# A selective-scan stage: one product with C for both feature halves, one GpSimd product of dx and B, and TensorE's side work one step earlier

## The chip, the core and the metric

The kernel runs on one core of one Trainium2 chip. Its engines are PE (TensorE, with PEld for its weight loads), DVE (VectorE), ACT (ScalarE), POOL (GpSimd) and SP (SyncE, which issues the DMAs here). The metric is device time in microseconds for the whole program. The program is eight stages of a network; the change is in one of them, the selective scan.

## The reference, cut to what matters

The stage is a Mamba block on 2048 tokens of width 128. It has 256 inner features and 16 states for each feature. For every state `s` and every feature, a recurrence runs over the tokens:

```python
def step(h, inp):
    x_t, d_t, B_t, C_t = inp
    dA = jnp.exp(d_t[:, :, None] * A[None, :, :])
    h = dA * h + (d_t * x_t)[:, :, None] * B_t[:, None, :]
    y_t = jnp.einsum('bds,bs->bd', h, C_t)
    return (h, y_t)
...
y = _selective_scan(x_ssm, delta, A, B, C, Dp)     # + x * Dp
y = y * _silu(z)
out = jnp.einsum('ble,de->bld', y, out_proj_w)
```

`x_ssm` comes from a convolution over four tokens and a SiLU, `delta`, `B` and `C` from projections of `x_ssm`, and `z` from a projection of the block's input.

## The kernel before

The tokens are cut into 4 chunks of 512 (`c`), and the 256 features into two halves of 128 partitions (`d` = 0, 1). A chunk has 16 steps, one for each state (`s`; `g = 16 c + s`). Every engine runs its own list in program order and waits on semaphores.

One step goes through the engines like this:

- ACT: `exp(delta * A)` of both halves into two PSUM banks (L1712). Then it saves the last column of the step before (`save`, L1690), and does the ACT part of the side work.
- SP: loads row `s` of B, spread over the partitions, into a ring of four tiles `b_rows` (L1454), and in five of the steps a row of C (L1460).
- POOL: `dbx = dx * b_rows`, one instruction for each half (L1520), into a ring of four tiles, which are two steps. A half's product waits until the scan two steps back is done.
- DVE: two scans (L1821), one for each half, from the exponential, `dbx` and the saved state into `h`, which has two buffers. Then the product of `h` with the row of C, which TensorE has spread over the partitions in a PSUM bank: `hc = h * C`, one instruction for each half (L1833).
- PE: for each half, `hc` is added into a PSUM bank by a matmul with the identity (`add_up`, L1572). Between the two halves' matmuls it spreads C's row for the next step (`spread_c`, L1565). There is one bank for C, so the spreading waits for the products of the step before.

In the steps 1, 3, 7, 9 and 11 (`LOW_STEPS`), POOL multiplies the second half of `h` with C instead (`read_out`, L1495, two steps later), and PE adds that (`add_low`, L1578). So 11 steps of a chunk have two products on DVE (called pair steps below), and 5 have one (single steps).

Around this, side work for this chunk, for the chunk before and for the chunk after is put into the steps by hand. On DVE, at the end of a step: `finish` (L1777, y times the gate of z, chunk before) in step 0, `add_out` (L1783, into the residual, chunk before) in step 2, `gate_z` (L1765) in 3 and 4, `gate_x` (L1759, chunk after) in 6 and 8, `take_delta` (L1769, chunk after) in 12 and 13. On PE, after the step's `add_up`s: `find_z` (L1543) in 0 and 2, `project_out` (L1589, chunk before) in 1, the convolution of the chunk after in 3 to 6 (`convolve`, L1381, two of its four matmuls in each), `project_x` (L1400) in 7 and 9, `project_dt` (L1553, L1555) in 8, 10 and 11, `add_skip` in 13 and 14. ACT and POOL have their parts of the gates between: ACT opens the gate of z in step 2, POOL sums it in step 4 (`sum_z`, L1487), and ACT closes it in step 3 or 4, ahead of the exponentials of the next step.

PSUM banks are shared, and that is where some of the waits come from: `convolve` of the chunk after writes the bank from which `add_out` reads, and waits for it; `project_x` reads `xs`, which `gate_x` writes; the first `add_up` of a chunk waits until `finish` has read the sums of the chunk before.

Of the kernel before, what the change touches and what calls it, by code (L numbers as in the profile page):

```python
# [1262 lines left out]
def selective_scan(core, early_ctx, ln, following):  # L1263
# [6 lines left out]
    LOW_STEPS, C_RING = (1, 3, 7, 9, 11), 3  # L1270
# [143 lines left out]
    def rest(ctx):  # L1414
# [8 lines left out]
        zs = [sb(f"zs{d}", [P, CH]) for d in range(ND)]  # L1423
# [5 lines left out]
        dx = [[sb(f"dx{i}{d}", [P, CH]) for d in range(ND)] for i in range(2)]  # L1429
# [4 lines left out]
        dbx = [sb(f"dbx{i}", [P, CH]) for i in range(RING)]  # L1434
        b_rows = [sb(f"b_rows{i}", [P, CH]) for i in range(RING)]
        h = [sb(f"h{i}", [P, ND, CH]) for i in range(2)]
        hc = [sb(f"hc{d}", [P, CH]) for d in range(ND)]
        state = sb("state", [P, DS, ND])
        yT = [sb(f"yT{d}", [P, CH]) for d in range(ND)]
# [3 lines left out]
        @block.sync  # L1443
        def _(sp):
            for c in range(NC_):
                cols = slice(c * CH, (c + 1) * CH)
                if c:
                    store_b(sp, c)
                sp.wait_ge(b_stored, 16 * (c + 1))
                for s in range(DS):  # L1450
                    g = c * DS + s
                    if g >= RING:
                        sp.wait_ge(dbx_done, (g - RING + 1) * ND)
                    sp.dma_start(b_rows[g % RING][:],  # L1454
                                 b_dram[s:s + 1, cols].to_broadcast([P, CH])).then_inc(b_loaded[g % RING], 16)
                    if s in LOW_STEPS:
                        k = low_before(g)
                        if k >= C_RING:
                            sp.wait_ge(low_done, k - C_RING + 1)
                        sp.dma_start(c_rows[k % C_RING][:],  # L1460
                                     b_dram[DS + s:DS + s + 1, cols].to_broadcast([P, CH])).then_inc(
                                         c_loaded[k % C_RING], 16)

        @block.gpsimd
        def _(pool):
# [6 lines left out]
            def join(c):  # L1472
                pool.wait_ge(cut_line, 3 * c + 2)
                if c:
                    pool.wait_ge(dbx_done, ((c - 1) * DS + DS - 1) * ND)
# [13 lines left out]
            def read_out(g):  # L1489
                k = low_before(g)  # L1490
                pool.wait_ge(c_loaded[k % C_RING], 16 * (k // C_RING + 1))
                pool.wait_ge(scanned, (g + 1) * ND)
                if k >= 2:
                    pool.wait_ge(low_summed, k - 1)
                nc.gpsimd.tensor_tensor(low[k % 2][:], h[g % 2][:, 1, :], c_rows[k % C_RING][:],  # L1495
                                        ALU.mult).then_inc(low_done, 1)

            def weigh(c, d):
                pool.wait_ge(delta_done, ND * c + d + 1)
                nc.gpsimd.tensor_tensor(dx[c % 2][d][:], delta[c % 2][d][:], xs[c % 2][d][:], ALU.mult).then_inc(dx_done, 1)  # L1500
# [7 lines left out]
            for c in range(NC_):  # L1508
                pool.wait_ge(dx_done, ND * (c + 1))
                for s in range(DS):  # L1510
                    g = c * DS + s
                    for d in range(ND):
                        u = g * ND + d
                        if d == 1 and s - 2 in LOW_STEPS:
                            read_out(g - 2)
                        if u >= RING:
                            pool.wait_ge(scanned, u - RING + 1)
                        if d == 0:
                            pool.wait_ge(b_loaded[g % RING], 16 * (g // RING + 1))
                        nc.gpsimd.tensor_tensor(dbx[u % RING][:], dx[c % 2][d][:], b_rows[g % RING][:],  # L1520
                                                ALU.mult).then_inc(dbx_done, 1)
                    if s in (4, 5):
                        sum_z(c, s - 4)
                    elif c + 1 < NC_:
                        if s in (6, 8):
                            sum_x(c + 1, s // 2 - 3)
                        elif s == 13:
                            cut(c + 1)
                        elif s == 14:
                            join(c + 1)  # L1530
                        elif s == 15:
                            weigh(c + 1, 0)
                            weigh(c + 1, 1)
# [3 lines left out]
        def _(pe):  # L1537
# [30 lines left out]
            def add_up(c, s, d):  # L1568
                if s == 0 and c:
                    pe.wait_ge(y_done, ND * (c - 1) + d + 1)  # L1570
                pe.wait_ge(hc_done, high_before(c * DS + s) + d + 1)
                nc.tensor.matmul(core.ps[:, Y_BANK + d, :], core.ident[:], hc[d][:],  # L1572
# [11 lines left out]
            def project_out(c):  # L1584
                pe.wait_ge(y_done, ND * (c + 1))
                pe.wait_ge(delta_done, min(ND * (c + 1) + 1, ND * NC_))
                for k in range(TPC):
                    for d in range(ND):
                        last = nc.tensor.matmul(core.ps[:, O_BANK, k * P:(k + 1) * P], yT[d][:, k * P:(k + 1) * P],  # L1589
# [13 lines left out]
            for c in range(NC_):  # L1603
                spread_c(c, 0)
                for s in range(DS):
                    if s:
# [6 lines left out]
                    if s in (0, 2):  # L1613
                        find_z(c, s // 2)
                    elif s == 1 and c:
                        project_out(c - 1)
                    elif c + 1 < NC_:
                        if s in (3, 4):
                            convolve(pe, c + 1, 0, range(0, 2) if s == 3 else range(2, DCONV))
                        elif s in (5, 6):  # L1620
                            convolve(pe, c + 1, 1, range(0, 2) if s == 5 else range(2, DCONV))
                        elif s == 7:
                            project_x(pe, c + 1, 0)
                        elif s == 8:
                            project_dt(c + 1, 0, 0)
                        elif s == 9:
                            project_x(pe, c + 1, 1)
                        elif s == 10:
                            project_dt(c + 1, 0, 1)
                        elif s == 11:  # L1630
# [12 lines left out]
        def _(act):  # L1643
# [43 lines left out]
            def save(c, s):  # L1687
                g = c * DS + s
                act.wait_ge(scanned, (g + 1) * ND)
                nc.scalar.copy(state[:, s, :], h[g % 2][:, :, CH - 1]).then_inc(saved, 1)  # L1690
# [57 lines left out]
        def _(dve):  # L1748
# [14 lines left out]
            def gate_z(c, d):  # L1763
                dve.wait_ge(z_gated, ND * c + d + 1)
                nc.vector.tensor_tensor(zs[d][:], core.ps[:, Z_BANKS[d], :], z_gate[d][:], ALU.mult).then_inc(zs_done, 1)  # L1765
# [6 lines left out]
            def finish(c):  # L1772
                for d in range(ND):
                    dve.wait_ge(summed, high_before(DS * (c + 1) - 1) + d + 1)
                    if c:
                        dve.wait_ge(out_done, c)
                    nc.vector.tensor_tensor(yT[d][:], core.ps[:, Y_BANK + d, :], zs[d][:], ALU.mult).then_inc(y_done, 1)  # L1777
# [28 lines left out]
            for c in range(NC_):  # L1806
                for s in range(DS):
                    g = c * DS + s
                    for d in range(ND):
                        u = g * ND + d  # L1810
                        dve.wait_ge(da_done, u + 1)
                        dve.wait_ge(dbx_done, u + 1)
                        if g >= 2 and d == 1 and (g - 2) % DS in LOW_STEPS:
                            dve.wait_ge(low_done, low_before(g - 2) + 1)
                        elif g >= 2:
                            dve.wait_ge(hc_done, high_before(g - 2) + d + 1)
                        if g >= 2:
                            dve.wait_ge(saved, g - 1)
                        if c and s < 2:
                            dve.wait_ge(saved, g)  # L1820
                        nc.vector.tensor_tensor_scan(out=h[g % 2][:, d, :], data0=core.ps[:, A_BANKS[d], :],  # L1821
                                                     data1=dbx[u % RING][:], initial=state[:, s, d:d + 1],
                                                     op0=ALU.mult, op1=ALU.add).then_inc(scanned, 1)
                    dve.wait_ge(c_spread, g + 1)
                    for d in range(ND):
# [1297 lines left out]
```

## Time and profile before

| what | value |
|---|---|
| time, median of 3 runs (lowest to highest) | 1595.23 us (1588.64 to 1595.8) |
| the profiled execution: time, span | 1593.81 us, 1592.1 us |
| the scan stage in the trace | 853 to 1104 us |
| PE, DVE, ACT, POOL busy over the whole span | 93%, 85%, 58%, 20% |
| mean granted clock of TensorE, whole span | 0.965 |

The span is the time from the first to the last instruction of the core; the program's time is 1.71 us longer. Busy shares are means over eight stages with different limits: POOL's 20% is the mean of stages in which it has nothing to do and of the scan stage, in which it is busy most of the time. A timeline row gives an instruction's start, its duration (of all of a run of like instructions, if it ends in x2 and more), and in brackets how long its engine stood idle before it and what ended that. Two DVE instructions in a row with no wait between them overlap in the records: the second starts a little before the first one's end.

### The profile page before, as it was taken

The page shows a single profiled execution, that of the slowest core. Times are in us where ns is not written, and L with a number is a line of the kernel's source. Part 1 is how long each engine was busy: PE and PEld are TensorE (multiplying, and loading weights), DVE is VectorE, ACT ScalarE, POOL GpSimd, SP SyncE. Part 2 cuts the span into 40 slices and gives each one's busy share as a digit, 9 for nine tenths or more (in the row PEclk, how much of TensorE's full clock was granted, in tenths as well). Part 3 has the DMA queues.
Part 4 walks back from the last instruction along what each step waited for, and adds up shares of the span by engine and source line. Part 5 has one row for each costly group of instructions (what it writes and reads, how often), then busy time and mean ns, then how long its engine had stood idle before and what let it go on. Part 6 is the DMA issues. An engine that isn't in the chain of part 4 may idle for free. (4 is left out here: it accounts for less than half of the span.)

```text
span 1592.1 us, 28331 instructions
## 1 busy us (share of the span) xinstructions
PE 1487.0 (93%) x10635; PEld 786.2 (49%) x10635; DVE 1345.6 (85%) x2432; ACT 930.0 (58%) x1755; POOL 317.4 (20%) x370
## 2 busy tenths in 40 slices
PE   7999999999999999899997988977999999989899
PEld 3122222222222222488873333333888877869787
DVE  7999999999999999376657999998776668877686
ACT  3189999999999999632235665754332342222232
POOL 4200000000000000000016889885000110020100
PEclk8599999999999999899999999999999999999899
DMA  3341110000000001000003233330000012300123
GB/s 104 125 144 31 30 34 29 25 25 25 26 25 26 26 25 55 6 1 1 1 3 93 80 88 96 89 95 23 1 1 1 1 35 75 108 1 1 54 88 101
DMA packets 44274, 71.55 MB, mean 45 GB/s; under 512 B 11764, under 2 KB 18981, under 8 KB 43434
## 3 DMA queue, kind: packets, MB, share of 16 engines
q1 hardware_dynamic: 44138, 69.75, 15.0%
q8 instruction: 84, 1.38, 0.4%
q14 instruction: 52, 0.43, 0.1%
HBM read 61.92 MB, written 6.88 MB: 43 GB/s over the span
## 5 line engine op out<-in xcount | busy, mean ns | idle before, releaser
L917 DVE TENSOR_REDUCE row_max<-ps 128x1 f32<-128x1024 f32 x512 | 583.4, 1212 | 10.6 <-PE ps L703 10.5
L823 ACT ACTIVATE probs<-ps 128x512 f32<-128x512 f32 x944 | 506.2, 595 | 51.9 <-PE ps L718 35.5
L703 PE MATMUL ps<-k_stack,q_stack 48*128 48x512 bf16 x1024 | 325.6, 401 | 10.9 <-DVE row_max L917 6.6
L644 PE MATMUL ps<-probs,v_head 128*16 128x256 f32 (+1 forms) x3920 | 316.2, 395 | 1.1 <-issue 1.1
L718 PE MATMUL ps<-q_stack,k_stack 51*128 51x512 bf16 x944 | 286.8, 384 | 0.0
L703 PEld LDWEIGHTS ps<-k_stack,q_stack 48*128 48x128 bf16 x1024 | 58.9, 95 | 249.0 <-DVE row_max L917 221.8
L1114 ACT ACTIVATE x_gate<-ps 128x512 f32<-128x512 f32 x128 | 76.5, 599 | 178.0 <-PE ps L131 178.0
L644 PEld LDWEIGHTS ps<-probs,v_head 128*16 128x16 f32 x3920 | 65.6, 94 | 199.4 <-issue 102.4
L1821 DVE TENSOR_TENSOR_SCAN s_h<-ps,s_state,s_dbx 128x512 f32<-128x512 f32 x128 | 156.7, 1265 | 7.8 <-ACT ps L1712 7.7
L1572 PE MATMUL ps<-s_hc,ident 128*128 128x512 f32 x216 | 119.8, 641 | 46.0 <-DVE s_hc L1833 40.7
L1520 POOL TENSOR_TENSOR s_dbx<-s_dx,s_b_rows 128x512 f32<-128x512 f32 x128 | 159.6, 1274 | 9.9 <-DVE s_h L1821 9.3
L1160 DVE TENSOR_TENSOR x_hidden<-x_gate,ps 128x512 f32<-128x512 f32 x128 | 87.0, 685 | 50.1 <-PE ps L131 38.5
L1712 ACT ACTIVATE ps<-s_delta,s_a_neg 128x512 f32<-128x512 f32 x128 | 86.5, 688 | 66.6 <-DVE s_h L1821 66.2
L1073 PEld LDWEIGHTS ps<-w_w,x_hidden 128*128 128x128 f32 x1024 | 122.7, 192 | 5.3 <-issue 1.5
L1073 PE MATMUL ps<-w_w,x_hidden 128*128 128x128 f32 x1024 | 125.0, 275 | 0.0
L2230 ACT ACTIVATE y_gate<-ps 128x512 f32<-128x512 f32 (+1 forms) x72 | 43.1, 598 | 119.1 <-PE ps L131 119.1
L129 PE MATMUL ps<-x_x_high,x_w_high 128*128 128x512 f32 x256 | 107.0, 418 | 1.1 <-DVE x_hidden L1160 1.1
L1171 DVE SCALAR_TENSOR_TENSOR x_res<-ps,x_probs,x_res 128x128 f32<-128x128 f32 x256 | 72.0, 344 | 42.3 <-PE ps L1073 41.9
L131 PE MATMUL ps<-x_x_low,x_w_high 128*128 128x512 f32 x256 | 101.6, 397 | 0.0
L130 PE MATMUL ps<-x_x_high,x_w_low 128*128 128x512 f32 x256 | 100.5, 393 | 0.0
L1572 PEld LDWEIGHTS ps<-s_hc,ident 128*128 128x128 f32 x216 | 39.5, 200 | 107.1 <-DVE s_hc L1833 78.0
L548 POOL TENSOR_TENSOR neg_max_parts<-neg_maxT,by_one 128x32 bf16<-128x32 f32 x16 | 4.0, 252 | 402.2 <-DVE neg_maxT L910 402.2
(357 smaller groups left out, 2091.5 us busy)
## 6 DMA issues: line engine op xcount, KB each, us to landing
s_b_rows<-s_b_dram SPq DMA_DIRECT2D x64, 256.0 KB, 3.3
y_spread<-y_probs_dram SPq DMA_DIRECT2D x128, 128.0 KB, 3.0
s_c_rows<-s_b_dram SPq DMA_DIRECT2D x20, 256.0 KB, 4.5
q_stack<-q_parts_dram SPq DMA_DIRECT2D x30, 96.0 KB
k_stack<-k_parts_dram SPq DMA_DIRECT2D x30, 96.0 KB
w_w<-w_dram SPq DMA_DIRECT2D x1, 2048.0 KB, 8.1
q_stack<-q_parts_dram SPq DMA_DIRECT2D x30, 64.0 KB
k_stack<-k_parts_dram SPq DMA_DIRECT2D x30, 64.0 KB
```

Of the source, the lines that this page charges most:

```text
L129: nc.tensor.matmul(bank, self.w_high[:, u, cols], self.x_high[:, chunk], start=True, stop=False)
L130: nc.tensor.matmul(bank, self.w_low[:, u, cols], self.x_high[:, chunk], start=False, stop=False)
L131: return nc.tensor.matmul(bank, self.w_high[:, u, cols], self.x_low[:, chunk], start=False, stop=True)
L644: last = nc.tensor.matmul(core.ps[32 * c:32 * c + VROWS, O_BANK, cut], v_head[buf][:, kt, :], probs[:, m % RING, c * CH:(c + 1) * CH][:, cut],
L703: last = nc.tensor.matmul(core.ps[:, 2 * b + r, :], qst[buf][0:KROWS, u * P:(u + 1) * P], kst[buf][0:KROWS, key:key + CH], start=True, sto ...
L718: nc.tensor.matmul(core.ps[:, S_BANK + n % S_RING, :], kst[buf][HALF:ROWS, kt * P:(kt + 1) * P], qst[buf][HALF:ROWS, c * CH:(c + 1) * CH], ...
L823: nc.scalar.activation(probs[:, us % RING, c * CH:(c + 1) * CH], core.ps[:, S_BANK + n % S_RING, :], ACT.Exp).then_inc(exp_done, 1)
L917: nc.vector.tensor_reduce(mx[:, head % 2, u, b:b + 1], core.ps[:, 2 * b:2 * b + 2, :], mybir.AxisListType.XY, ALU.max).then_inc(max_done, 1)
L1073: last = nc.tensor.matmul(core.ps[:, DOWN + n % 2, k * P:(k + 1) * P], hidden[n % 2][:, half, k * P:(k + 1) * P], w["w3"][:, e, half, :], ...
L1520: nc.gpsimd.tensor_tensor(dbx[u % RING][:], dx[c % 2][d][:], b_rows[g % RING][:], ALU.mult).then_inc(dbx_done, 1)
L1572: nc.tensor.matmul(core.ps[:, Y_BANK + d, :], core.ident[:], hc[d][:], start=s == 0, stop=s == DS - 1).then_inc(summed, 1)
L1821: nc.vector.tensor_tensor_scan(out=h[g % 2][:, d, :], data0=core.ps[:, A_BANKS[d], :], data1=dbx[u % RING][:], initial=state[:, s, d:d + 1 ...
```

## The change

- `h` has three buffers in place of two, and `dbx` is a ring of three pairs in place of four single tiles.
- POOL makes `dbx` for both halves in one instruction, with B's row read twice. The first scan of a step waits for that one instruction. `read_out` comes after it; before, it stood between the two halves' products.
- DVE multiplies both halves with C in one instruction (`read_high`) in the pair steps. In every step this waits for both scans of the step, and for all the `add_up`s of the step before.
- `finish` is one instruction for both halves, into `zs`, and stands in step 1 between the two scans; before, it stood at the end of step 0.
- PE's side work: both `find_z` in step 0; `project_out` in step 1, now ahead of that step's `add_up`s; and the convolution, `project_x` and `project_dt` each one step earlier (2 to 5, 6 and 8, 7, 9 and 10).

The side work on DVE, ACT and POOL keeps its steps. The diff, cut to its core:

```diff
+    H_RING, PAIR_RING = 3, 3
@@ POOL
-                    for d in range(ND):
-                        u = g * ND + d
-                        if d == 1 and s - 2 in LOW_STEPS:
-                            read_out(g - 2)
-                        if u >= RING:
-                            pool.wait_ge(scanned, u - RING + 1)
-                        if d == 0:
-                            pool.wait_ge(b_loaded[g % RING], 16 * (g // RING + 1))
-                        nc.gpsimd.tensor_tensor(dbx[u % RING][:], dx[c % 2][d][:], b_rows[g % RING][:],
-                                                ALU.mult).then_inc(dbx_done, 1)
+                    if g >= PAIR_RING:
+                        pool.wait_ge(scanned, (g - PAIR_RING + 1) * ND)
+                    pool.wait_ge(b_loaded[g % RING], 16 * (g // RING + 1))
+                    nc.gpsimd.tensor_tensor(dbx[g % PAIR_RING][:], dx[c % 2][:],
+                                            b_rows[g % RING][:].unsqueeze(1).to_broadcast([P, ND, CH]),
+                                            ALU.mult).then_inc(dbx_done, 1)
+                    if s - 2 in LOW_STEPS:
+                        read_out(g - 2)
@@ PE
                 if c or s:
-                    pe.wait_ge(hc_done, high_before(c * DS + s))
+                    pe.wait_ge(hc_done, c * DS + s)
...
                 for s in range(DS):
+                    if s == 1 and c:
+                        project_out(c - 1)
                     if s:
                         add_up(c, s - 1, 0)
                         spread_c(c, s)
...
-                    if s in (0, 2):
-                        find_z(c, s // 2)
-                    elif s == 1 and c:
-                        project_out(c - 1)
+                    if s == 0:
+                        for d in range(ND):
+                            find_z(c, d)
                     elif c + 1 < NC_:
-                        if s in (3, 4):
-                            convolve(pe, c + 1, 0, range(0, 2) if s == 3 else range(2, DCONV))
-                        elif s in (5, 6):
-                            convolve(pe, c + 1, 1, range(0, 2) if s == 5 else range(2, DCONV))
-                        elif s == 7:
+                        if s in (2, 3):
+                            convolve(pe, c + 1, 0, range(0, 2) if s == 2 else range(2, DCONV))
+                        elif s in (4, 5):
+                            convolve(pe, c + 1, 1, range(0, 2) if s == 4 else range(2, DCONV))
+                        elif s == 6:
                             project_x(pe, c + 1, 0)
...
@@ DVE
+            def read_high(g):
+                dve.wait_ge(c_spread, g + 1)
+                dve.wait_ge(scanned, (g + 1) * ND)
+                if g:
+                    dve.wait_ge(summed, high_before(g))
+                if g % DS in LOW_STEPS:
+                    nc.vector.tensor_tensor(hc[:, 0, :], h[g % H_RING][:, 0, :], core.ps[:, C_BANK, :],
+                                            ALU.mult).then_inc(hc_done, 1)
+                else:
+                    nc.vector.tensor_tensor(hc[:], h[g % H_RING][:],
+                                            core.ps[:, C_BANK, :].unsqueeze(1).to_broadcast([P, ND, CH]),
+                                            ALU.mult).then_inc(hc_done, 1)
...
-                        dve.wait_ge(dbx_done, u + 1)
+                        if d == 0:
+                            dve.wait_ge(dbx_done, g + 1)
...
+                        if d == 1 and s == 1 and c:
+                            finish(c - 1)
                         nc.vector.tensor_tensor_scan(...).then_inc(scanned, 1)
-                    dve.wait_ge(c_spread, g + 1)
-                    for d in range(ND):
-                        u = g * ND + d
-                        if d == 1 and s in LOW_STEPS:
-                            continue
-                        dve.wait_ge(scanned, u + 1)
-                        last = g - 2 if d == 1 and (g - 1) % DS in LOW_STEPS else g - 1
-                        if g:
-                            dve.wait_ge(summed, high_before(last) + d + 1)
-                        nc.vector.tensor_tensor(hc[d][:], h[g % 2][:, d, :], core.ps[:, C_BANK, :],
-                                                ALU.mult).then_inc(hc_done, 1)
-                    if s == 0 and c:
-                        finish(c - 1)
-                    elif s == 2 and c:
+                    read_high(g)
+                    if s == 2 and c:
                         add_out(c - 1)
```

## Rows read from the trace of the kernel before

**Rows 1.** Windows, the scan stage: length, busy PE, PEld, DVE, ACT, POOL, clock, DMA.

```profile
853.00:1104.00 251.00, 205.24 (x493) 82.07 (x493) 236.06 (x269) 151.78 (x302) 217.83 (x180) 0.96 0.31 83
```

**Rows 2.** Waits of DVE in the scan stage: us in total, times, longest.

```profile
DVE s_h L1821 <- ACT ps L1712: 7.7, 5, 2.2
DVE s_hc L1833 <- PE ps L1565: 4.8, 5, 1.3
DVE s_zs L1765 <- ACT s_z_gate L1673: 1.0, 1, 1.0
...
DVE s_hc L1833 <- PE ps L1572: 0.7, 3, 0.2
```

**Rows 3.** Timeline of DVE, steps 10 to 12 of chunk 1: start, us, instruction.

```profile
957.28 2.45 DVE L1821 TENSOR_TENSOR_SCAN s_h<-ps,s_state,s_dbx 128x512 f32<-128x512 f32 x2
959.65 1.25 DVE L1833 TENSOR_TENSOR s_hc<-s_h,ps 128x512 f32<-128x512 f32 x2
960.83 2.45 DVE L1821 TENSOR_TENSOR_SCAN s_h<-ps,s_state,s_dbx 128x512 f32<-128x512 f32 x2
963.20 0.66 DVE L1833 TENSOR_TENSOR s_hc<-s_h,ps 128x512 f32<-128x512 f32 x1
963.77 2.45 DVE L1821 TENSOR_TENSOR_SCAN s_h<-ps,s_state,s_dbx 128x512 f32<-128x512 f32 x2
967.50 1.28 DVE L1833 TENSOR_TENSOR s_hc<-s_h,ps 128x512 f32<-128x512 f32 x2 [1.28 <-PE ps L1565]
```

**Rows 4.** Timeline of DVE ahead of the stage: the second waits for the first.

```profile
843.99 0.68 DVE L1787 TENSOR_TENSOR s_rest<-s_full,s_bc 96x512 f32<-96x512 f32 x1
...
844.71 0.42 DVE L1789 CAST s_mid<-s_rest 96x512 bf16<-96x512 f32 x1
```

**Rows 5.** Groups by line and form, DVE, same operation at two lengths.

```profile
L917 DVE TENSOR_REDUCE row_max<-ps 128x1 f32<-128x1024 f32 x512 | 583.4, 1212 | 10.6 <-PE ps L703 10.5
...
L2050 DVE TENSOR_REDUCE l_k_maxima<-ps 128x1 f32<-128x512 f32 x4 | 2.7, 686 | 0.2 <-PE ps L1931 0.2
```

**Rows 6.** Groups by line and form, GpSimd.

```profile
L1520 POOL TENSOR_TENSOR s_dbx<-s_dx,s_b_rows 128x512 f32<-128x512 f32 x128 | 159.6, 1274 | 9.9 <-DVE s_h L1821 9.3
...
L2609 POOL TENSOR_TENSOR g_span<-g_span 128x512 f32<-128x512 f32 x1 | 1.9, 1901 | 0.1
L2609 POOL TENSOR_TENSOR g_span<-g_f 128x1024 f32<-128x1024 f32 x1 | 1.9, 1893 | 4.8 <-DVE g_f L2834 4.8
```

**Rows 7.** Timeline of DVE and TensorE, step 14 of chunk 0.

```profile
909.31 1.26 DVE L1833 TENSOR_TENSOR s_hc<-s_h,ps 128x512 f32<-128x512 f32 x2
...
910.03 1.12 PE L1572 MATMUL ps<-s_hc,ident 128*128 128x512 f32 x2 [0.22 <-DVE s_hc L1833]
...
910.99 0.38 PE L1565 MATMUL ps<-s_bc,w_pick 96*128 96x512 bf16 x1
...
911.21 1.02 PE L1572 MATMUL ps<-s_hc,ident 128*128 128x512 f32 x2
```

**Rows 8.** Timeline, the last output projection.

```profile
1104.80 2.05 PE L1589 MATMUL ps<-w_out_proj,s_yT 128*128 128x128 f32 x16 [0.78 <-DVE s_yT L1777]
```

**Rows 9.** Timeline of DVE, product of step 1 of chunk 1.

```profile
925.29 0.66 DVE L1833 TENSOR_TENSOR s_hc<-s_h,ps 128x512 f32<-128x512 f32 x1
```

**Rows 10.** Timeline of DVE, scans of step 4 of chunk 0.

```profile
871.31 2.46 DVE L1821 TENSOR_TENSOR_SCAN s_h<-ps,s_state,s_dbx 128x512 f32<-128x512 f32 x2 [2.18 <-ACT ps L1712]
```

**Rows 11.** Timeline, GpSimd and DVE at the first step.

```profile
852.96 3.73 POOL L1520 TENSOR_TENSOR s_dbx<-s_dx,s_b_rows 128x512 f32<-128x512 f32 x3
...
854.38 2.48 DVE L1821 TENSOR_TENSOR_SCAN s_h<-ps,s_state,s_dbx 128x512 f32<-128x512 f32 x2
```

**Rows 12.** Timeline of DVE, last product and last addition to the residual.

```profile
1101.32 1.26 DVE L1833 TENSOR_TENSOR s_hc<-s_h,ps 128x512 f32<-128x512 f32 x2
...
1106.89 0.69 DVE L1783 TENSOR_TENSOR x_res<-x_res,ps 128x512 f32<-128x512 f32 x1 [0.75 <-PE ps L1589]
```

**Rows 13.** Windows, 4 us of chunk 3 (columns as in Rows 1).

```profile
1066.00:1070.00 4.00, 4.00 (x7) 1.62 (x5) 3.77 (x5) 1.63 (x4) 2.58 (x3) 0.53 0.23 55
```

More of the change, by code:

```diff
@@ L1422, in rest @@
         neg_b = sb("neg_b", [P, ND])
-        zs = [sb(f"zs{d}", [P, CH]) for d in range(ND)]
+        zs = sb("zs", [P, ND, CH])
         x_gate = [sb(f"x_gate{d}", [P, CH]) for d in range(ND)]
@@ L1428, in rest @@
         delta = [[sb(f"delta{i}{d}", [P, CH]) for d in range(ND)] for i in range(2)]
-        dx = [[sb(f"dx{i}{d}", [P, CH]) for d in range(ND)] for i in range(2)]
+        dx = [sb(f"dx{i}", [P, ND, CH]) for i in range(2)]
         rest_bc = sb("rest", [96, CH])
@@ L1433, in rest @@
         low = [sb(f"low{i}", [P, CH]) for i in range(2)]
-        dbx = [sb(f"dbx{i}", [P, CH]) for i in range(RING)]
+        dbx = [sb(f"dbx{i}", [P, ND, CH]) for i in range(PAIR_RING)]
         b_rows = [sb(f"b_rows{i}", [P, CH]) for i in range(RING)]
-        h = [sb(f"h{i}", [P, ND, CH]) for i in range(2)]
-        hc = [sb(f"hc{d}", [P, CH]) for d in range(ND)]
+        h = [sb(f"h{i}", [P, ND, CH]) for i in range(H_RING)]
+        hc = sb("hc", [P, ND, CH])
         state = sb("state", [P, DS, ND])
-        yT = [sb(f"yT{d}", [P, CH]) for d in range(ND)]
         block = ctx.enter_context(nc.Block())
@@ L1494, in read_out @@
                     pool.wait_ge(low_summed, k - 1)
-                nc.gpsimd.tensor_tensor(low[k % 2][:], h[g % 2][:, 1, :], c_rows[k % C_RING][:],
+                nc.gpsimd.tensor_tensor(low[k % 2][:], h[g % H_RING][:, 1, :], c_rows[k % C_RING][:],
                                         ALU.mult).then_inc(low_done, 1)
@@ L1588, in project_out @@
                     for d in range(ND):
-                        last = nc.tensor.matmul(core.ps[:, O_BANK, k * P:(k + 1) * P], yT[d][:, k * P:(k + 1) * P],
+                        last = nc.tensor.matmul(core.ps[:, O_BANK, k * P:(k + 1) * P], zs[:, d, k * P:(k + 1) * P],
                                                 w["out_proj"][:, d, :], start=d == 0, stop=d == ND - 1)
@@ L1612, in _ @@
                             add_low(c, s - 2)
-                    if s in (0, 2):
-                        find_z(c, s // 2)
-                    elif s == 1 and c:
-                        project_out(c - 1)
+                    if s == 0:
+                        for d in range(ND):
+                            find_z(c, d)
                     elif c + 1 < NC_:
-                        if s in (3, 4):
-                            convolve(pe, c + 1, 0, range(0, 2) if s == 3 else range(2, DCONV))
-                        elif s in (5, 6):
-                            convolve(pe, c + 1, 1, range(0, 2) if s == 5 else range(2, DCONV))
+                        if s in (2, 3):
[3 more added lines that the diff above has]
+                        elif s == 6:
+                            project_x(pe, c + 1, 0)
                         elif s == 7:
-                            project_x(pe, c + 1, 0)
+                            project_dt(c + 1, 0, 0)
                         elif s == 8:
-                            project_dt(c + 1, 0, 0)
+                            project_x(pe, c + 1, 1)
                         elif s == 9:
-                            project_x(pe, c + 1, 1)
+                            project_dt(c + 1, 0, 1)
                         elif s == 10:
-                            project_dt(c + 1, 0, 1)
-                        elif s == 11:
                             for d in range(ND):
@@ L1772, in finish @@
             def finish(c):
-                for d in range(ND):
[L1774 to L1777, printed above, removed]
+                dve.wait_ge(summed, high_before(DS * (c + 1)))
+                if c:
+                    dve.wait_ge(out_done, c)
+                nc.vector.tensor_tensor(zs[:], core.ps[:, Y_BANK:Y_BANK + ND, :], zs[:], ALU.mult).then_inc(y_done, 1)
+            def read_high(g):
[10 more added lines that the diff above has]
+                                            ALU.mult).then_inc(hc_done, 1)
             def add_out(c):
@@ L1811, in _ @@
                         dve.wait_ge(da_done, u + 1)
-                        dve.wait_ge(dbx_done, u + 1)
[L1813 to L1820, printed above, removed]
@@ L1835, in _ @@
-                    if s == 0 and c:
-                        finish(c - 1)
-                    elif s == 2 and c:
+                        if d == 0:
+                            dve.wait_ge(dbx_done, g + 1)
+                        if g >= H_RING:
+                            dve.wait_ge(hc_done, g - H_RING + 1)
+                            dve.wait_ge(saved, g - H_RING + 1)
+                            if d == 1 and (g - H_RING) % DS in LOW_STEPS:
+                                dve.wait_ge(low_done, low_before(g - H_RING) + 1)
@@ new lines, in _ @@
+                        if d == 1 and s == 1 and c:
+                            finish(c - 1)
+                        nc.vector.tensor_tensor_scan(out=h[g % H_RING][:, d, :], data0=core.ps[:, A_BANKS[d], :],
+                                                     data1=dbx[g % PAIR_RING][:, d, :], initial=state[:, s, d:d + 1],
+                                                     op0=ALU.mult, op1=ALU.add).then_inc(scanned, 1)
+                    read_high(g)
+                    if s == 2 and c:
```

25 lines of the change are left out of this document (12 added, 13 removed).

## The prediction, made before the changed kernel ran

> **What bounds the kernel now.** I read first the windows of the scan stage. In its 251 us DVE is busy 236, POOL 218, PE 205 and ACT 152 [rows 1]. The reader is to see that DVE sets the pace with POOL close behind, so an edit counts where it makes DVE's list longer or makes DVE wait.
>
> Second, DVE's waits: 14.2 us in the loop, of which 7.7 are scans waiting for ACT's exponentials, 1.0 a gate of z and 5.5 (4.8 and 0.7) products waiting for TensorE [rows 2].
>
> Third, DVE's timeline. With nothing waited for, two scans take 2.37 us from their start to the product's start, the pair of products 1.18 and a single one 0.57: a pair step is 3.55, a single step 2.94 [rows 3]. Each instruction starts about 0.08 ahead of the recorded end of the one before. The last row shows the wait that matters here: after step 11, in which TensorE had `project_dt` behind its `add_up`s, the next product stood 1.28 us for the spread row of C [rows 3]. TensorE works in order, and side work in front of an `add_up` delays DVE.
>
> Fourth, TensorE's own rhythm. DVE's first half product ends near 909.97, and `add_up` starts 0.06 later. It takes 0.96 until the spreading starts, that takes 0.22 until the next `add_up` starts, and records run on 0.16 past that (0.38 against 0.22); an `add_up` with its weights there takes 0.86 (1.02 less 0.16) [rows 7].
>
> **The change, part by part.**
>
> *The product behind its own scans.* Before, the first half's product read a scan that had ended a whole scan earlier. Now each product waits for the scan just in front of it. Ahead of the stage, a DVE instruction that waits for its forerunner starts 0.04 after that one's end (843.99 + 0.68 = 844.67, start 844.71) [rows 4], where one without a wait starts 0.08 ahead of it [rows 3]. That is 0.12 in each of 64 steps: +7.7.
>
> The Trainium skill, VectorE: DVE Perf Modes, in "The DRAIN you can't avoid", says the opposite: chained operations cost the same with a semaphore after each, and one should save operations, not semaphores. By it this term is nothing and the sum some 6 us lower. The trace's 0.04 behind against 0.08 ahead disagrees, so I keep 0.12 and leave the rule a rival.
>
> *One product for two.* On DVE, a reduction over 512 more elements from PSUM costs 1212 − 686 = 526 ns more [rows 5]. So the pair takes 0.66 + 0.53 = 1.19, a pitch of 1.11 against 1.18: −0.07 in 11 steps of 4 chunks, −3.1; three merged `finish` −0.2. Bounds: two whole instructions, 1.32 (+0.13 × 44 = +5.7 on the sum), and 2 × 0.526 = 1.05 (−6.2). I take 1.19, the same engine's slope.
>
> *What the pair product does to TensorE's slack.* Let E be a pair product's end. TensorE starts `add_up` at E + 0.05; both `add_up`s and the spreading end at E + 0.05 + 0.96 + 0.22 + 1.02 = E + 2.25. The next product now needs all of that, because it waits for both sums. DVE could start it at E − 0.08 + 2.45 + 0.04 = E + 2.41. So 0.1 us is left. Before, TensorE began 0.6 earlier, with the first half, and the first product needed one sum and the spreading, at about E + 0.8: 1.5 us were left. Side work that ends late now shows on DVE, and the moves make it late:
>
> - *Step 1, three chunks.* `project_out` waits for `finish`, with `add_up`(0) and the spreading for step 1 queued behind it. It takes 2.05 − 0.16 = 1.89 [rows 8]. From `finish`'s end F: 0.05 + 1.89 + 0.86 + 0.22 + 1.02 + 0.04 = F + 4.1. DVE has one scan to do in that time and is ready at F − 0.08 + 1.27 + 0.04 = F + 1.2. A wait of 2.9 × 3 = +8.6. Before, `project_out` stood behind the `add_up`s, and the same product shows no wait [rows 9].
> - *Step 3, chunks 1 and 2.* The convolution, now in step 2, waits for `add_out` at the end of DVE's step 2; the two `add_up`s of step 2 are behind it. From `add_out`'s end: 0.15 + 1.72 (two matmuls of 0.86) + 2.10 + 0.04 = 4.0, against 2.4 for two scans and the wait. 1.6 × 2 = +3.2.
> - *Steps 7 and 9, three chunks.* `project_x`, now in 6 and 8, waits for `gate_x` at the end of that step on DVE. From `gate_x`'s end 0.05 + 0.96 + 2.10 + 0.04 = 3.15 against 2.4: 0.74 × 6 = +4.5.
> - *Steps 6 and 11, three chunks.* A convolution half with `add_low` in front of it, and three matmuls of `project_dt`, reach past the product: I count 0.4 and 0.7, × 3 = +3.2.
>
> Together 19.5 us of new waits on TensorE.
>
> *What goes.* The 5.5 us of waits on TensorE are replaced by these. The exponentials were late because ACT stood behind a gate of z for which POOL was late. In chunks 1 to 3 DVE now comes to step 4 later by 2.9 to 4.5 us, while ACT and POOL do not, so that chain is hidden. In chunk 0 nothing delays DVE earlier and POOL has as much to do ahead of its sum; the 2.2 us there [rows 10] stay. −14.2 + 2.2 = −12.0.
>
> *POOL's pairs.* Two products have a pitch of 2.49 (3.73 for three) [rows 11]. One instruction lies between 1.89 (the strided 1024 elements) and 3.80 (twice the slowest 512) [rows 6]; I take 2.49, since the work on each element is the same. POOL's other work is 218 − 160 = 58 us, so it becomes the bound only above (265 − 58)/64 = 3.2 us a pair. Between, it costs nothing: the ring of three pairs lets POOL be a step further ahead, and DVE's longer steps cover it. Only the first scan feels it: it can't start before the whole pair, +1.1 [rows 11]. `read_out` moves behind a product of 1.25 us; its sum is added two steps later, which covers that.
>
> *The end.* The last `finish` waits for both sums and is 1.19 long before `project_out` starts. By E + 2.07 + 1.19, then 2.05 and 0.08, the last `add_out` starts at E + 5.4, against 1106.89 − 1102.58 = 4.3 before [rows 12]: +1.1.
>
> *At nothing:* the third buffer of `h` (no scan waited for ACT's saving or for `read_out`); SP's loads, which wait for the same step's product as before; the earlier `find_z`, since ACT opens the gate in the same step.
>
> **Sum.** 7.7 − 3.1 − 0.2 + 19.5 − 12.0 + 1.1 + 1.1 = +14.1 on the profiled execution's 1593.81 us: 1607.9. That execution is 0.1% under the median of 1595.23, and the three runs spread over 0.5% (1588.64 to 1595.8), which is about what can be told from no change.
>
> **The rivals.**
>
> *A free own-scan wait.* If DVE runs through without the gap, 7.7 falls away in the steps that do not wait for TensorE (about 49 of 64, −5.9); in the others the TensorE wait grows by as much. 1602. For it: POOL and DVE both have long lists without a gap; against it: rows 4. This is the skill's rule above, told as this kernel's mechanism.
>
> *Not slower: the gate chain was the loss.* The place is step 4, where ACT's exponentials come late. If POOL's longer lead takes off all of the 14.2 us, and TensorE's waits stay at the 5.5 of before, the sum is 7.7 − 3.3 − 14.2 + 5.5 + 2.2 = −2.1, 1592. For it: all four chunks have that stall, and TensorE has 46 us without matmuls in the stage [rows 1]. Against it: the idle time lies in other steps than the side work. It decides from the point where new TensorE waits are under about 8 us in place of 19.5.
>
> *POOL becomes the bound.* Place: the pair product with a row read twice. At 3.80 us each [rows 6], POOL needs 64 × 3.80 + 58 = 301 us against 251: 1644. Against it: 128 ordinary products here average 1274 ns, and the 1901 is a single record.
>
> *The clock.* In 1066 to 1070 TensorE was granted 0.53 of its clock, its lower level of 1.2 GHz, and was busy all the time [rows 13]; it had come out of an idle stretch. With half the clock the chain behind a pair product is about 2 us longer, and there is no slack now. Three or four such steps more than are hidden: 1615. Against it: the long idle stretches at step 4 become shorter.
>
> **How the numbers follow.** Chances: the forecast 0.68 (its own range 1602 to 1614, by the bounds of the product and of the steps 6 and 11), the free wait 0.10, the gate chain 0.10, the clock 0.08, POOL 0.04. Predicted is 1608. The range of 1596 to 1616 leaves out most of the gate chain, POOL and a little of the clock. Slower by over 0.5% is above 1603: nearly all of the forecast, the clock and POOL, and a third of the free wait, 0.75. Within 0.5%: the rest of the free wait, most of the gate chain and the forecast's low end, 0.21. Faster 0.04.
>
> **What would show it.** DVE's waits for TensorE near 20 us, at the steps named: about 2.9 ahead of step 1's product in three chunks, 1.6 ahead of step 3's in two, 0.7 ahead of 7's and 9's. The pair product near 1.19 us in 44 instances, starting 0.04 after the scan's end. Waits for exponentials at step 4 only in chunk 0. POOL's pair under 2.6 us. The stage near 265 us. I am wrong if step 1's product starts without a wait, or if the pair product or POOL's pair lies outside its bounds.

## The result, and the profile after

The changed kernel takes 1628.34 us (median of 4 runs, 1626.34 to 1630.79) against 1592.53 for the kernel before: a ratio of 1.0223, 95% interval 1.0199 to 1.0247. It is slower, as forecast, but by 35.8 us and not by 14. The profiled execution took 1626.34 us, its span is 1624.6, which is 32.5 longer than before.

DVE's waits in the scan stage, after (us in total, times, longest):

```profile
DVE s_hc L1784 <- PE ps L1569: 36.6, 16, 4.7
DVE s_hc L1787 <- PE ps L1569: 6.3, 10, 1.2
```

Before there were 5.5 us on TensorE and 8.7 on ACT [rows 2]; now there are 43 on TensorE (L1569 is `add_up`), and none on ACT. The 16 waits ahead of single products (L1784) are the large ones.

One place in full, steps 5 to 7 of chunk 0, from the timeline of DVE and TensorE, other engines left out:

```profile
875.08 2.45 DVE L1833 TENSOR_TENSOR_SCAN s_h<-ps,s_state,s_dbx 128x512 f32<-128x512 f32 x2
...
877.62 1.22 DVE L1787 TENSOR_TENSOR s_hc<-s_h,ps 128x1024 f32<-128x1024 f32 x1
878.76 2.45 DVE L1833 TENSOR_TENSOR_SCAN s_h<-ps,s_state,s_dbx 128x512 f32<-128x512 f32 x2
...
882.61 0.74 DVE L1757 SCALAR_TENSOR_TENSOR s_xs<-ps,w_conv_b,s_x_gate 128x512 f32<-128x512 f32 x1
883.27 2.45 DVE L1833 TENSOR_TENSOR_SCAN s_h<-ps,s_state,s_dbx 128x512 f32<-128x512 f32 x2
...
883.41 1.87 PE L1400 MATMUL ps<-s_xs,w_x_bc 128*96 128x512 f32 x2 [2.07 <-DVE s_xs L1757]
...
885.08 1.91 PE L1569 MATMUL ps<-s_hc,ident 128*128 128x512 f32 x2
...
886.78 0.49 PE L1562 MATMUL ps<-s_bc,w_pick 96*128 96x512 bf16 x1
887.12 1.02 PE L1569 MATMUL ps<-s_hc,ident 128*128 128x512 f32 x2
...
888.27 0.69 DVE L1784 TENSOR_TENSOR s_hc<-s_h,ps 128x512 f32<-128x512 f32 x1 [2.56 <-PE ps L1569]
```

The reader is to see three things. First, TensorE stands idle for 2.07 us in front of `project_x` (L1400) until `gate_x` (L1757) is done, with the `add_up`s of step 6 queued behind it: that is the forecast's mechanism. Second, `project_x` and the `add_up` after it then take 1.87 and 1.91, where an `add_up` took 1.02 before [rows 7] and the next one at 887.12 takes 1.02 again. Third, the pair product starts 0.09 after the scans' end (875.08 + 2.45 = 877.53), and a pair step without a wait is 3.68 (875.08 to 878.76) against 3.55 [rows 3].

The windows say why those two matmuls are long (length, then busy us of PE, PEld, DVE, ACT, POOL, then TensorE's granted clock, DMA share, GB/s):

```profile
855.00:1138.00 283.00, 220.85 (x488) 87.76 (x489) 236.21 (x218) 152.68 (x302) 206.47 (x115) 0.90 0.24 73
...
884.00:886.00 2.00, 2.00 (x4) 0.73 (x3) 1.72 (x2) 1.65 (x4) 1.10 (x1) 0.50 0.68 173
886.00:888.00 2.00, 2.00 (x5) 0.57 (x3) 0.00 (x0) 1.09 (x3) 2.00 (x2) 0.75 0.02 5
888.00:890.00 2.00, 2.00 (x5) 0.78 (x5) 1.73 (x2) 0.00 (x0) 2.00 (x3) 1.00 0.14 50
```

TensorE's granted clock is 0.50 behind the idle stretch, its lower level of 1.2 GHz, and 1.00 again 3 us later. Over the stage it is 0.90 where it was 0.96 [rows 1]. In windows of 2 us I count 16 such low stretches in the stage, against 4 before. TensorE stood idle for 2.0 us or more 19 times, and 16 of these stretches were followed by the lower clock. Eight of the 16 end in work that the change moved, five in `project_x`, two in the convolution and one in `project_out`, and the costly waits stand behind them: 2.56 and 2.55 at steps 7 and 9, 3.30 and 3.50 at step 3, 4.66 in step 1 of chunk 3. The other eight end in an `add_up`, one at the stage's start and seven after a single product, where TensorE waits for the whole pair product of the next step. Step 8 of chunk 3, before and after, shows that this idle time grew too:

```profile
1078.41 1.12 PE L1572 MATMUL ps<-s_hc,ident 128*128 128x512 f32 x2 [1.60 <-DVE s_hc L1833]
```

```profile
1110.83 1.13 PE L1569 MATMUL ps<-s_hc,ident 128*128 128x512 f32 x2 [2.34 <-DVE s_hc L1787]
```

**The account.** From the first scan's start to the last product's end the stage was 248.2 us and is now 283.0: +34.8. DVE's own steps are longer by 0.13 in 44 pair steps and by 0.20 (3.14 against 2.94) in 20 single steps, +9.7. Of the 43.0 us before a product, 0.09 each time is in that already: 26 waits, 40.6 net, against 6.1 for the 8 of before, counted alike: +34.5. The waits on ACT go, −9.2 counted alike, and three merged `finish`es give −0.2. Ahead of the stage the first scan starts 4.62 us after the start of the last `take_delta`, where it was 3.54, and behind it the last `add_out` comes 1.1 later: both 1.1 as forecast. The rest of the program happens to be 4.5 shorter in this execution.

The GpSimd pair, from the groups by line and form, lies inside its bounds [rows 6], and no scan inside the stage waits for it:

```profile
L1514 POOL TENSOR_TENSOR s_dbx<-s_dx,s_b_rows 128x1024 f32<-128x1024 f32 x64 | 150.1, 2355 | 18.7 <-DVE s_h L1833 18.0
```

### The profile page after: what moved, and what is told of

It reads as the page before. It is cut to its first block and busy times, and to the rows that moved or that the text cites. A ratio compares the mean times of both kernels' runs of the same rounds, so it can differ in the third digit from the quotient of the medians.

```text
span 1624.6 us, 28133 instructions
## 1 busy us (share of the span) xinstructions
PE 1501.1 (92%) x10635; PEld 787.9 (48%) x10635; DVE 1348.9 (83%) x2384; ACT 931.0 (57%) x1755; POOL 308.9 (19%) x306
## 5 line engine op out<-in xcount | busy, mean ns | idle before, releaser
L1569 PE MATMUL ps<-s_hc,ident 128*128 128x512 f32 x216 | 130.0, 690 | 39.8 <-DVE s_hc L1787 35.2
L1514 POOL TENSOR_TENSOR s_dbx<-s_dx,s_b_rows 128x1024 f32<-128x1024 f32 x64 | 150.1, 2355 | 18.7 <-DVE s_h L1833 18.0
L1569 PEld LDWEIGHTS ps<-s_hc,ident 128*128 128x128 f32 x216 | 43.6, 215 | 104.0 <-DVE s_hc L1787 54.5
```

The lines of the kernel that those rows point to most:

```text
L1514: nc.gpsimd.tensor_tensor(dbx[g % PAIR_RING][:], dx[c % 2][:], b_rows[g % RING][:].unsqueeze(1).to_broadcast([P, ND, CH]), ALU.mult).then_ ...
```

## The experiments

Each time is a median of 4 or 5 runs, beside the kernel before on the same chip (1592.7 to 1593.3); the changed kernel is 1628.34. "Stage" is first scan's start to last product's end in the profiled execution. What lies outside the stage took 1341.6 us in the changed kernel's profiled execution, the least of all, and up to 1349.1 in the others, of which the edits explain 2.2 at most; so a part is priced by its stage too.

**1. Is it TensorE's moves, or the pair product?** The change with TensorE's side work put back:

```diff
-                    if s == 1 and c:
-                        project_out(c - 1)
...
-                    if s == 0:
-                        for d in range(ND):
-                            find_z(c, d)
+                    if s in (0, 2):
+                        find_z(c, s // 2)
+                    elif s == 1 and c: project_out(c - 1)
...            # convolve 2..5 -> 3..6, project_x 6, 8 -> 7, 9, project_dt 7, 9, 10 -> 8, 10, 11
```

> The changed kernel, with only TensorE's side work put back to the steps of before (project_out behind step 1's add_ups, the second find_z in step 2, convolution in 3 to 6, project_x in 7 and 9, project_dt in 8, 10 and 11). If the moves are the cause of DVE's 43 us of waits for TensorE, those fall to about 10 (1.0 in step 1 of three chunks, because finish still stands in step 1, 1.3 behind project_dt in three, and the start), and the time to about 1598, some 0.4% above the kernel before: what is left is the wait for the own scans. If instead the pair product with its wait for both sums is the cause, wherever the side work stands, the waits stay above 30 us and the time above 1618.

1609.18 us, ratio 1.0103 (1.0086 to 1.0121); stage 261.1, waits on TensorE 20.0. The moves on top of the rest cost 19 us in time and 21.9 in the stage, over half. But 16 us stay, where I had expected 5: step 1 waits 2.2, 2.9 and 1.2 and not 1.0, two of them behind a low stretch, and the own steps are 9.7 longer. Neither theory alone was right.

**2. The moves alone**, on the kernel before (the reverse of the diff above, products in halves):

```diff
+                    if s == 1 and c:
+                        project_out(c - 1)
...
-                    if s in (0, 2):
-                        find_z(c, s // 2)
-                    elif s == 1 and c:
-                        project_out(c - 1)
+                    if s == 0:
+                        for d in range(ND):
+                            find_z(c, d)
...            # convolve, project_x and project_dt as in the change
```

> The kernel before, with only TensorE's side work moved as in the change; DVE's products, GpSimd and the rings are those of before. By full-clock arithmetic DVE's first product needs only one add_up and the spreading, so steps 1 and 3 wait about 0.8 us (five places) and steps 7 and 9 not at all: +4, about 1596. If TensorE's idle time in front of project_x and the convolution also brings the lower clock, those places cost about 1.5 us more each: about 1605. If the merged product is the whole cause, no change: 1592.

1602.25 us, 1.0062 (1.0041 to 1.0084). Its waits:

```profile
DVE s_hc L1834 <- PE ps L1565: 17.3, 19, 2.5
```

The moves hurt half products too, but 9 us and not 19: a half product needs one `add_up` and the spreading (the wait is now for L1565, the spreading), so part of the delay is hidden. The time lies between the two expected, for another reason than either: steps 8, 10 and 11 wait about 0.98, 0.6 and 0.39 in three chunks and step 4 waits 0.85 in two, where nothing was counted. The low clock is there too, in seven stretches, but only some 5 of the 17.3 us stand behind it.

**3. The wait for the own scans alone**, on the kernel before:

```diff
-                        dve.wait_ge(scanned, u + 1)
+                        dve.wait_ge(scanned, (g + 1) * ND)
```

> The kernel before, with one wait changed: DVE's first product of a step waits for both scans of its step and not for the first alone. This prices the wait for the own scans by itself. By the gap read in the changed kernel (0.09 after the scan's end where it was 0.08 ahead) 0.17 us in 64 steps: +10.9, about 1603, DVE's waits unchanged. By my forecast's 0.12: +7.7, 1600. By the rule that a wait behind one's own instruction is free: 1592.

1601.87 us, 1.0059 (1.004 to 1.0078); stage +8.9. Two steps of its timeline of DVE:

```profile
877.46 2.45 DVE L1821 TENSOR_TENSOR_SCAN s_h<-ps,s_state,s_dbx 128x512 f32<-128x512 f32 x2
880.00 1.29 DVE L1833 TENSOR_TENSOR s_hc<-s_h,ps 128x512 f32<-128x512 f32 x2
881.21 2.45 DVE L1821 TENSOR_TENSOR_SCAN s_h<-ps,s_state,s_dbx 128x512 f32<-128x512 f32 x2
```

Scans to product is 2.54 where it was 2.37: 0.17 a step, 10.9 in 64. The half products take a little more (1.21 to the next scan against 1.18 [rows 3]), and shorter waits bring some back: 5.7 us on ACT where there were 8.7 [rows 2], the gate of z among them. So the price of waiting for the instruction just in front is real and on the path. The Trainium skill's statement that the semaphore costs nothing extra (VectorE: DVE Perf Modes, "The DRAIN you can't avoid") rests there on a chain of copies; for this kernel's scans it does not hold, and the measured 8.5 us decide.

**4. GpSimd's part alone**, on the kernel before (`dbx` in pairs, a ring of three, `read_out` behind it):

```diff
-                    for d in range(ND):
...
-                        nc.gpsimd.tensor_tensor(dbx[u % RING][:], dx[c % 2][d][:], b_rows[g % RING][:],
-                                                ALU.mult).then_inc(dbx_done, 1)
+                    if g >= PAIR_RING:
+                        pool.wait_ge(scanned, (g - PAIR_RING + 1) * ND)
...
+                    nc.gpsimd.tensor_tensor(dbx[g % PAIR_RING][:], dx[c % 2][:],
+                                            b_rows[g % RING][:].unsqueeze(1).to_broadcast([P, ND, CH]),
+                                            ALU.mult).then_inc(dbx_done, 1)
...
-                        dve.wait_ge(dbx_done, u + 1)
+                        if d == 0:
+                            dve.wait_ge(dbx_done, g + 1)
```

> The kernel before, with GpSimd's part of the change alone: one product of dx and B for both halves, a ring of three pairs, read_out behind it. If GpSimd's longer lead takes ACT's late exponentials away, DVE's 7.7 us of waits for ACT fall to about 2 and the first scan starts 1.1 later: about 1588. If the ring gives no lead there, 1593. A GpSimd pair is 2.36 us as in the changed kernel either way.

1586.65 us, 0.9959 (0.9943 to 0.9975); stage 240.9. DVE waits for ACT 2.3 us and not 7.7. So this part of the change is a gain of 7 us. The edit has three pieces, the ring of three, the pair product (2.36 us for two halves that had a pitch of 2.49) and `read_out` behind it; which of them brings GpSimd's lead was not tested apart.

**5. Is the low clock a cause, or a by-product?** The change, with filler matmuls where TensorE would stand idle:

```diff
+            def fill(c, count):
+                for _ in range(count):
+                    nc.tensor.matmul(core.ps[:, Y_BANK, :], zeros[:], bc[c % 2][:], start=False, stop=False)
...
+                        if s == 2 and c:
+                            fill(c, 12)
...
+                            fill(c, 8)
                             project_x(pe, c + 1, 0)
```

> The changed kernel, with filler matmuls (a weight of zeros, added into the open Y bank, so the sums stay the same) where TensorE stands idle: eight of 0.22 us ahead of both project_x and twelve ahead of the convolution of chunks 1 and 2. They end before what TensorE waits for there, so no work is moved or delayed. If the lower clock behind that idle time is what makes the waits 2.55 us at steps 7 and 9 and 3.4 at step 3, they fall to the full-clock 0.75 and 1.6: some 12 us less, about 1616. If the order of the queue alone makes them, nothing changes: 1628.

1620.73 us, 1.0182 (1.0162 to 1.0202). The waits at the filled places fell to what the full clock gives, in chunk 1 for instance:

```profile
941.87 0.69 DVE L1795 TENSOR_TENSOR s_hc<-s_h,ps 128x512 f32<-128x512 f32 x1 [1.80 <-PE ps L1571]
...
967.11 0.69 DVE L1795 TENSOR_TENSOR s_hc<-s_h,ps 128x512 f32<-128x512 f32 x1 [0.86 <-PE ps L1571]
```

All six at steps 7 and 9 are 0.86, both at step 3 are 1.80. DVE's waits for TensorE fell from 43.0 to 31.5 and the stage from 283.0 to 271.8, which is about the 12 us expected. The time gained only 7.6, since what lies outside the stage was 4.7 longer in the profiled execution than in the changed kernel's. At places without fillers the low stretches stayed or grew (4.66 in step 1 of chunk 3, 1.43 in step 13 of chunk 0).

**6. All of TensorE's idle time filled:**

```diff
+            FILL = {2: 12, 6: 8, 8: 8, 12: 8, 14: 2, 15: 5}
+            LAST_FILL = {2: 10, 3: 3, 4: 10, 5: 2, 6: 6, 7: 4, 8: 10, 10: 10, 12: 10, 14: 2, 15: 5}
...                    # fillers by step; chunk 0 has its own count in steps 1 and 2, and
...                    # 16 in step 0; 8 stand ahead of project_out in step 1, into the free output bank
```

> The changed kernel, with filler matmuls in every longer idle stretch of TensorE in the scan stage (zeros added into the open Y bank, or written to the free output bank in steps 0 and 1), counted so that they end before what TensorE waits for. All the work of the change stays where the change put it. If the lower clock is the second half of the loss, the granted clock stays near 1.00 through the stage, DVE's waits for TensorE fall from 43 us to the full-clock 21 or so (2.9 in step 1, 1.8 in step 3, 0.86 in 7 and 9, 0.96 in 11), and the time comes to about 1607, which is the forecast's full-clock sum. If the fillers only shift the low stretches, the waits stay above 30 us and the time above 1616.

1608.42 us, 1.0095 (1.0078 to 1.0112); stage 263.2. Windows over its stage, then its waits:

```profile
855.00:1119.00 264.00, 244.08 (x715) 99.72 (x714) 237.05 (x219) 152.70 (x302) 207.19 (x116) 1.00 0.28 79
```

```profile
DVE s_hc L1805 <- PE ps L1571: 20.6, 14, 3.0
...
DVE s_hc L1808 <- PE ps L1571: 0.8, 3, 0.3
```

TensorE does more work, its clock is 1.00 from end to end, and the stage is 19.8 us shorter with every piece of the change where the change put it. The waits left are 2.99 at step 1 (three times), 1.8 at step 3 (two), 0.86 at steps 7 and 9 (six), 0.96 at step 11 (three) and 0.26 at step 6 (three).

**7. One move put back at a time.** `project_x` and `project_dt`, in the changed kernel:

```diff
-                        elif s == 6:
+                        elif s == 7:
                             project_x(pe, c + 1, 0)
-                        elif s == 7:
+                        elif s == 8:
                             project_dt(c + 1, 0, 0)
...                # likewise project_x 8 -> 9, project_dt 9, 10 -> 10, 11
```

> The changed kernel, with project_x and project_dt alone put back by one step (7 and 9; 8, 10 and 11); the convolution, find_z and project_out stay moved. If project_x behind gate_x is the largest single cost, the 13.6 us of waits at steps 7 and 9 go and about 2 come back behind project_dt at step 12: about 1617. If the waits only move on to other steps, less than 4 us change: above 1624.

1620.78 us, 1.0179 (1.0163 to 1.0195), between the two times expected; stage 273.7. The waits at steps 7 and 9 are gone, 1.68 came behind `project_dt` three times; and step 1, which had 2.99 in two of its chunks, now waits about 4.65 in all three, behind a low stretch of its own. `project_out`, in the changed kernel:

```diff
-                    if s == 1 and c:
-                        project_out(c - 1)
                     if s:
...
+                    elif s == 1 and c:
+                        project_out(c - 1)
```

> The changed kernel, with project_out alone put back behind step 1's add_ups. At full clock the wait ahead of step 1's product falls from 2.9 to 1.07 (add_up, spreading and add_up behind finish) in three chunks: 5.5 us less, about 1622. If TensorE's idle stretch ahead of finish then brings the lower clock there, the waits stay near 2.5 and the time falls by 1 to 2 us: about 1627.

1621.55 us, 1.018 (1.0165 to 1.0195), the time expected, but by luck: the stage is 270.9, 12 us shorter and not 5.5, and what lies outside it was 7.5 longer in the profiled execution. Step 1 waits 1.82, 1.20 and 2.08, and two of the six waits at steps 7 and 9 are long, not five. A part put back moves the low stretches about, so such differences don't add up to the whole.

**8. The products alone**: experiment 1's diff, and `finish` as before:

```diff
-                        if d == 1 and s == 1 and c:
-                            finish(c - 1)
...
                     read_high(g)
-                    if s == 2 and c:
+                    if s == 0 and c:
+                        finish(c - 1)
+                    elif s == 2 and c:
```

> The changed kernel with TensorE's side work and finish at the places of before, so that of the change only the products remain: one of dx and B, one with C in each pair step, and the rings. Against the run with the side work put back (1609), the waits in step 1 behind finish (6 us in three chunks) go: about 1603. Against the GpSimd part alone (1587) what is left, some 16 us, is the price of the one product with C: about 9.5 for the gap behind its own scans, and the rest TensorE waits that the first half product used to hide.

1599.06 us, 1.004 (1.0024 to 1.0055), 4 us under the time expected; stage 253.7. So the whole change can be built up from experiment 4's stage of 240.9: the one product with C (here with the third buffer of `h` and the one `finish` for both halves) adds 12.8, putting `finish` into step 1 adds 7.4 (261.1, experiment 1), and TensorE's moves add 21.9 (283.0).

**9. A version that beats both.** Experiment 4 with one matmul group moved:

```diff
                         elif s == 10:
                             project_dt(c + 1, 0, 1)
+                            project_dt(c + 1, 1, 0)
                         elif s == 11:
-                            for d in range(ND):
-                                project_dt(c + 1, 1, d)
+                            project_dt(c + 1, 1, 1)
```

> The kernel with GpSimd's part alone (1587 us), and one of the three matmul groups of project_dt moved from step 11 to step 10. There DVE waits 1.3 us behind project_dt in three chunks. If that is only the length of the queue in step 11, the waits go and the time is about 1583. If step 10 has no room, they move to step 11 and the time stays 1587.

1583.72 us, 0.9945 (0.9927 to 0.9963), 9.5 us under the kernel before. The waits behind `project_dt` fell from 1.3 to 0.27, and the stage is 237.9, 3.0 under experiment 4's; in time the intervals of the two experiments overlap. The longest wait left on TensorE, 1.3, stands in step 10 of chunk 3:

```profile
DVE s_h L1820 <- ACT ps L1710: 2.3, 4, 1.5
DVE s_hc L1832 <- PE ps L1563: 2.1, 4, 1.3
```

## Why the prediction was right in its direction and wrong in its size

*The step that failed* is the price of TensorE's waits: "Together 19.5 us of new waits on TensorE" was worked out from matmuls at the full clock. At the full clock it was right: experiment 6 has 21.4, 19.9 without the 0.09 of each. The changed kernel has 43.0, since TensorE stood idle for two microseconds or more 19 times, and behind 16 of these stretches its clock was half, mostly just where DVE was waiting. Experiment 6 shows this: it fills the idle time and leaves each move where it was, and the waits fall by 20.7 us net; experiment 5 shows it place by place. Of the 21.5 us by which the waits exceed those of experiment 6, 13.3 stand behind moved work that waited for DVE's side work, and 8.2 behind an `add_up` that waited for DVE's product.

That experiment 6's time of 1608.42 is the 1608 of the forecast is in part luck. DVE's own steps cost 5.1 us more than forecast (below), its waits on ACT (the gate's among them) fell by 7.9 and not by the 6.5 that the −12.0 held, and the runs differ by more than what is left: the profiled execution of experiment 6 took 1610.17.

I had the clock as a rival, at 0.08 and with a price of 7 us. Its argument against, "the long idle stretches at step 4 become shorter", looked at the stretch that goes and not at the ones that my own steps make: in front of `project_x`, the convolution and `project_out` I had worked out that TensorE waits for DVE, without asking what the work after such a wait would cost. That the pair product itself keeps TensorE idle for longer after a single product was not in the sum at all.

*The own-scan wait* was taken at 0.12 and is 0.17: the start lies 0.09 behind the scan's end where it was 0.08 ahead. The rival "a free own-scan wait" is refuted by experiment 3. So, for this kernel, is the Trainium skill's rule behind it. *One product for two* was sized at −0.07 a pair step and is −0.04 (1.14 against 1.18). Both terms together, 7.7 − 3.1 = 4.6, measured 9.7.

*The places* were right: steps 1, 3, 6, 7, 9 and 11, and nothing at the others at full clock. At step 1 the wait is 2.99 for the forecast 2.9, at step 3 1.8 for 1.6, at 7 and 9 0.86 for 0.74, at 11 0.96 for 0.7.

*What goes*: all 14.2 us went and not 12.0; step 1 of chunk 0 waits 2.03 behind the low clock at the stage's start, so the exponentials of its step 4 are in time too. This hangs on the low clock: in experiment 6, without that wait, 0.8 us on ACT is back at the same step.

*GpSimd* was costed at nothing inside the change beyond the 1.1 us of the first scan, and both stand. By itself its part is worth 7 us, which the sum held in the "−12.0": what the rival "the gate chain was the loss" supposed, that GpSimd's lead takes off the stalls at step 4, holds for most of them in experiment 4 (8.7 to 2.3 us), which does not move TensorE's work.

Open: why 3 of the 19 idle stretches (at 929, 1003 and 1032 us) were not followed by the low clock, and which of the low stretches fall at random. That the low places move from one variant to the next was seen, not explained.

## What to carry to other kernels

Where an engine in order waits for a side result, count what is queued behind that wait, and for TensorE price that queue at both levels of its clock: here 16 of 19 idle stretches of two microseconds and more had the lower one behind them. Before merging two instructions into one, ask what each half let start early: here the first half's product hid a scan's end, an `add_up` and a spreading, and the merger saved 0.04 us a pair step for it. A change of several parts can hold a gain: GpSimd's part was worth 7 us by itself.

## What the runs showed of the hardware that was not expected

Filler matmuls on zeros, which bring the matmul records of its stage to 715 from the changed kernel's 488, made the changed kernel 20 us faster: 1608.42 against 1628.34. One GpSimd product over 1024 elements took 2.36 us, where two of 512 had a pitch of 2.49 [rows 11], although one operand is read twice. A DVE instruction that waits for its forerunner starts 0.09 us behind the end of a scan, and 0.04 behind that of the shorter operations ahead of the stage [rows 4].
